# Recommendation tower on one core: ScalarE takes row numbers off the ids in place, one-hots compare with a constant, layer 2's activation stands earlier in ScalarE's order

## The chip, the core and the metric

The kernel runs on one core of one Trainium2 chip. The core's engines work side by side from queues of their own and meet at semaphores: TensorE (PE in the rows; PEld is its weight loads), VectorE (DVE), ScalarE (ACT), GpSimd (POOL, which here only issues the indirect gathers) and SyncE (SP, which issues the plain DMAs). The metric is the device time of one execution in microseconds (us).

## What is computed

A batch of 2048 items. For each item 26 rows of 128 numbers are looked up in 26 tables, and together with the item's dense row they make 27 vectors. All pairs of vectors are multiplied (351 dot products), and a three-layer network runs over the result:

```
e = jnp.stack([tbl_0[ids[:, 0]], ..., tbl_25[ids[:, 25]]], axis=1)
all_vecs = jnp.concatenate([dense_proj[:, None, :], e], axis=1)        # 2048 x 27 x 128
interactions = jnp.einsum('bnd,bmd->bnm', all_vecs, all_vecs)
interact_flat = interactions[:, rows, cols]                           # upper triangle, 351
z = jnp.concatenate([dense_proj, interact_flat], axis=1)
h = jnp.concatenate([z, r_dense_proj], axis=1)
h = jnp.maximum(h @ W_top1 + b_top1, 0.0)     # 607 x 512
h = jnp.maximum(h @ W_top2 + b_top2, 0.0)     # 512 x 256
y = h @ W_top3                                # 256 x 1
```

## The kernel before

The batch is cut into 16 tiles of 128 items, and two tiles make a pair (8 pairs of 256 items). Tile t = 2 * pair + j, with j = 0 or 1.

**Lookups by matmul.** Eleven tables have 1000 rows. These lie in SBUF whole, as a high and a low part (`look_hi`, `look_lo`): row r of a table is on partition r // 8, in chunk r % 8. For one table and one pair, DVE makes eight one-hot matrices of 125 x 256, one for each chunk: element (p, b) is 1 where the id of item b is row 8 p + chunk. They are made in two units of four (`make_unit`, L592), one instruction each (L599), by comparing the ids, which a DMA broadcasts to all partitions as int32 (`step_ids`), with a column of row numbers (`row_no`, 128 x 8). PE then multiplies a unit's four chunks by the high and the low part (L378, L380): 8 matmuls a unit, 22 units a pair. Tile j = 0 of a pair makes and uses the 12 units of tables 0 to 5 of the *next* pair, tile j = 1 the 10 units of tables 6 to 10. The one-hots have 6 slots, so DVE is at most 5 or 6 units ahead of PE. ACT copies what has been looked up out of PSUM (`take_looked`, L717: L728, L734, L738, L740) and merges it into the tile's vectors (L748).

**The other 15 tables** are gathered by POOL with indirect DMAs (L316, 240 of them), turned by PE (L333) and copied by ACT (L572). `gram` (L450) multiplies the vectors, DVE turns the result (`turn`, L576: L579, L585, L588), PE turns the pairs once more (`pairs_out`, L385: L391), and ACT copies them (L698).

**The network** runs once a pair, a pair behind: `layer1` (L422) half in tile j = 0 and half in tile j = 1, `layer2` (L429) in the middle of tile j = 1, `layer3` (L440) at its end. ACT does the activations: `relu1` (L702), `relu2` (L706 and L707), `result` (L713).

**Order.** Each engine's order is written out by hand, tile by tile (`tile` in each engine's block); waits on semaphores tie them together. In the order of ACT, a tile copies groups 0 and 1 of the next tile's gathered rows, then pairs, dense rows and merges, `unit(3)`, group 2 of the rows ("third copy of rows"), `unit(7)`, group 3, and in tile j = 1 after that `relu2` and the last unit. The order of PE in tile j = 1: layer 1's second half, units and turns, first half of `gram`, layer 2, units and turns of groups 2 and 3, more units, second half of `gram`, layer 3. In the next tile j = 0, PE does two units, turns groups 0 and 1 and the dense rows, and then `pairs_out`, which waits for DVE's `turn` of the tile before; in DVE's order this `turn` stands behind the first 6 of 12 units of tile j = 0.

**Start.** Before tile 0 the eleven tables come in one after another by DMA (`load_table`), each behind the 128 KB of its ids (`load_first_ids`). ACT makes the high part (`take_high`, L789), DVE the one-hots and the low part (`take_low`, L609); tables 8 to 10 are first used unsplit (L375). Pairs 1 to 6 then run in a loop (`Fori(1, pairs - 1)`), and the last pair is written out. The ids of a later step come by `load_step` (SP, L244: 768 or 640 KB), once DVE has used up those in the buffer.

Of the kernel before, what the change touches and what calls it, by code (L numbers as in the profile page):

```python
# [33 lines left out]
F32 = mybir.dt.float32  # L34
# [65 lines left out]
def build(nc, dense, ids, look_ids, tables, look_tables, w1_dense, w1_pairs, b1, w2, b2, w3,  # L100
# [7 lines left out]
    with ExitStack() as ctx:  # L108
# [26 lines left out]
        row_no = sb("row_no", [P, LOOK_CH])  # L135
# [45 lines left out]
        gathered = [[sem(f"gathered{j}_{h}") for h in range(2)] for j in range(2)]  # L181
        first_ids_in = [sem(f"first_ids_in{f}") for f in range(LOOKUPS)]
# [47 lines left out]
        with nc.Block() as block:  # L230

            @block.sync
            def _(sp):
# [5 lines left out]
                def load_step(a, pair):  # L239

                    lo, hi = TABLES_OF[a]
                    sp.wait_ge(onehot_made, unit_count(pair - 1, 2 * hi - 1))
                    src = look_ids[lo:hi, bass.ds(pair * PAIR, PAIR)]
                    sp.dma_start(step_ids[a][:, :, :],  # L244
                                 src.unsqueeze(0).broadcast_to([P, hi - lo, PAIR])).then_inc(step_ids_in[a], 16)
# [44 lines left out]
                with sp.Fori(2, pairs) as r:  # L290
                    load_step(0, r)
                    load_step(1, r)
                    load_dense(2 * r, 0)
                    load_dense(2 * r + 1, 1)
                sp.wait_ge(y_out, 16 * (pairs + 1))
# [279 lines left out]
            def _(dve):  # L575
# [15 lines left out]
                def make_unit(a, pair, g, f, half):  # L591
# [5 lines left out]
                    for c in range(UNIT_CH):  # L597
                        ch = half * UNIT_CH + c
                        last = nc.vector.tensor_scalar(  # L599
                            onehot[:, SLOT[g], c, :], step_ids[a][0:LOOK_K, f - TABLES_OF[a][0], :],  # L600
                            row_no[0:LOOK_K, ch:ch + 1], None, ALU.is_equal)
# [10 lines left out]
                def tile(t, j, pair, first=False, look=True):  # L612
# [8 lines left out]
                    if look:  # L621
                        dve.wait_ge(step_ids_in[j], 16 * (pair + 1))
# [13 lines left out]
                dve.wait_ge(row_no_in, 16)  # L636
                for s in range(2):
                    for g, f, half in units(s):
                        if half == 0:
                            dve.wait_ge(first_ids_in[f], 16)  # L640
# [37 lines left out]
            def _(act):  # L678
# [71 lines left out]

                def tile(t, j, pair, first=False, mlp=True, look=True):
# [20 lines left out]
                    unit(3)  # L772
                    copy(n, k, 2)
# [6 lines left out]
                    if mlp and j == 1:  # L780
                        relu2(pair - 1)
# [9 lines left out]
                act.dma_start(row_no[:, :], row_numbers).then_inc(row_no_in, 16)  # L791
# [3 lines left out]
                ahead = LOOKUPS // 2  # L795
                for k in range(ahead):
                    take_high(k)
                for s in range(2):
                    for i, (g, f, half) in enumerate(units(s)):
# [8 lines left out]
                        if half == 1 and f + ahead < LOOKUPS:  # L808
                            take_high(f + ahead)
                tile(0, 0, 0, first=True, mlp=False)  # L810
# [64 lines left out]
```

## Times and profile before

| what | value |
|---|---|
| runs of the kernel before | 455.69, 456.03, 465.37 us; median 456.03 |
| the profiled execution | 457.95 us, its span 455.8 us |
| granted TensorE clock, mean over the span | 0.933 of full speed |
| busy over the span: PE | 385.5 us (85%) |
| PEld | 347.8 us (76%) |
| DVE | 254.1 us (56%) |
| ACT | 146.5 us (32%) |
| POOL | 230.8 us (51%) |
| chain that ended last | PE 72%, issue 10%, another core or an unknown queue 6%, DMA 3%, ACT 3%, SPq 3%, DVE 2% |

A row of the profile names the line of the kernel, the engine, the operation, what it writes and reads, and how often. Times are from the start of the span. In a timeline, the square brackets say how long the engine sat idle before the row, and what released it. "issue" is a wait for nothing that the profile shows, and "remote" is a releaser that it can't name. Full clock is 2.4 GHz (1.00 in the rows), half is 1.2 GHz (0.50).

### The profile page before, as it was taken

How to read it: one execution, taken by the hardware profiler on the slowest of the kernel's cores; microseconds unless marked ns; L12 is line 12 of the kernel's file. 1: busy time of each engine (PE TensorE's matmuls, PEld its weight loads, DVE VectorE, ACT ScalarE, POOL GpSimd, SP SyncE). 2: the span in 40 equal slices, each digit the busy share in tenths (PEclk: the TensorE clock that was granted, in tenths of full speed). 3: DMA queues.
4: the chain of work that ended last, by engine and by line, in shares of the span. 5: the costliest groups of instructions: out<-in, count | busy, mean ns of one | idle time of the engine just before them, and what ended most of it. 6: DMA issues, size and time to landing. Idle time of an engine off the chain costs nothing.

```text
span 455.8 us, 14934 instructions
## 1 busy us (share of the span) xinstructions
PE 385.5 (85%) x6224; PEld 347.8 (76%) x6224; DVE 254.1 (56%) x767; ACT 146.5 (32%) x265; POOL 230.8 (51%) x244
## 2 busy tenths in 40 slices
PE   0779858778898879997889799997999799997977
PEld 0779737767797779895879789885988689885865
DVE  5997729575654375466655466457754457441110
ACT  2264111321513233233424233233504224234422
POOL 4456737566555446545555556555455456551000
PEclk9979969898899989998999979997999979997999
DMA  8999812333251714324141714424151511110000
GB/s 195 239 249 209 233 41 59 98 59 87 61 94 46 91 45 66 84 47 92 42 102 40 104 46 60 91 51 87 41 106 37 95 54 40 40 35 19 3 3 0
DMA packets 25441, 36.37 MB, mean 80 GB/s; under 512 B 5378, under 2 KB 19594, under 8 KB 25417
## 3 DMA queue, kind: packets, MB, share of 16 engines
q1 hardware_dynamic: 17577, 20.27, 24.5%
q0 software_dynamic: 7680, 15.74, 12.7%
q8 instruction: 18, 0.29, 0.3%
q14 instruction: 6, 0.05, 0.0%
q10 hardware_dynamic: 160, 0.01, 0.0%
HBM read 35.99 MB, written 0.01 MB: 79 GB/s over the span
## 4 chain that ended last, share of the span: by engine, by line
PE 72%; issue 10%; another core or an unknown queue 6%; DMA 3%; ACT 3%; SPq 3%; DVE 2%; DVEq 0%; ACTq 0%
PE hid L422 11%; PE gram L450 9%; PE look_ps L378 8%; PE look_ps L380 7%; PE vec_act L333 6%; PE look_odd L380 5%; PE look_odd L378 5%; PE hid L429 5%; PE hid L378 4%; PE hid L380 3%; DMA table_raw<-tbl 3%; PE small L440 2%; DVE onehot L599 2%; PE look_odd L375 2%
## 5 line engine op out<-in xcount | busy, mean ns | idle before, releaser
L316 POOL DMA_INDIRECT vecs<-tbl,ids_sb x240 | 230.6, 961 | 181.2 <-issue 98.7
L599 DVE TENSOR_SCALAR onehot<-step_ids,row_no 125x256 fp32r<-125x256 int32 x704 | 209.8, 360 | 149.1 <-PE look_ps L380 48.2
L378 PE MATMUL look_ps<-onehot,look_hi 125*128 125x256 f32 x312 | 88.2, 313 | 8.4 <-issue 4.5
L380 PE MATMUL look_ps<-onehot,look_lo 125*128 125x256 f32 x312 | 83.5, 298 | 5.4 <-issue 5.3
L572 ACT COPY vecs_T<-vec_act 128x512 f32<-128x512 f32 x64 | 37.9, 600 | 138.7 <-remote 72.3
L450 PE MATMUL gram<-vecs_T 128*27 128x26 f32 x4096 | 52.6, 196 | 27.2 <-issue 27.2
L450 PEld LDWEIGHTS gram<-vecs_T 128*27 128x27 f32 x4096 | 45.4, 107 | 37.1 <-issue 33.4
L378 PEld LDWEIGHTS look_ps<-onehot,look_hi 125*128 125x128 f32 x312 | 64.6, 207 | 10.5 <-issue 5.7
L380 PEld LDWEIGHTS look_ps<-onehot,look_lo 125*128 125x128 f32 x312 | 64.6, 207 | 6.2 <-issue 6.0
L378 PE MATMUL look_odd<-onehot,look_hi 125*128 125x256 f32 x240 | 64.0, 300 | 3.3 <-issue 3.2
L380 PE MATMUL look_odd<-onehot,look_lo 125*128 125x256 f32 x240 | 60.2, 284 | 2.6 <-issue 2.5
L378 PE MATMUL hid<-onehot,look_hi 125*128 125x256 f32 x128 | 41.4, 347 | 11.4 <-DMA ident<-identity 10.8
L380 PEld LDWEIGHTS look_odd<-onehot,look_lo 125*128 125x128 f32 x240 | 45.8, 191 | 4.7 <-issue 4.1
L378 PEld LDWEIGHTS look_odd<-onehot,look_hi 125*128 125x128 f32 x240 | 45.8, 191 | 3.3 <-issue 2.9
L378 PEld LDWEIGHTS hid<-onehot,look_hi 125*128 125x128 f32 x128 | 30.5, 238 | 15.8 <-DMA ident<-identity 10.8
L422 PE MATMUL hid<-pairs_T,w_sb 117*128 117x256 f32 x168 | 40.9, 378 | 0.0
L333 PE MATMUL vec_act<-ident,vecs 128*128 128x128 f32 x240 | 39.1, 288 | 2.1 <-DMA vecs<-tbl,ids_sb 2.1
L380 PE MATMUL hid<-onehot,look_lo 125*128 125x256 f32 x128 | 38.5, 325 | 0.0
L422 PEld LDWEIGHTS hid<-pairs_T,w_sb 117*128 117x128 f32 x168 | 31.8, 189 | 4.5
L333 PEld LDWEIGHTS vec_act<-ident,vecs 128*128 128x128 f32 x240 | 29.9, 149 | 3.3 <-DMA vecs<-tbl,ids_sb 2.3
L380 PEld LDWEIGHTS hid<-onehot,look_lo 125*128 125x128 f32 x128 | 30.5, 238 | 0.0
L702 ACT ACTIVATE h_T<-hid 128x512 f32<-128x512 f32 x14 | 8.4, 598 | 65.0 <-remote 34.8
(80 smaller groups left out, 320.5 us busy)
## 6 DMA issues: line engine op xcount, KB each, us to landing
step_ids<-look_ids SPq DMA_DIRECT2D x7, 768.0 KB
table_raw<-tbl SPq DMA_DIRECT2D x11, 448.0 KB
step_ids<-look_ids SPq DMA_DIRECT2D x7, 640.0 KB
vecs<-tbl,ids_sb POOLq DMA_INDIRECT x240
step_ids<-look_ids SPq DMA_DIRECT2D x11, 128.0 KB, 9.6
vecs<-dense SPq DMA_DIRECT2D x16, 64.0 KB
table_raw<-tbl SPq DMA_DIRECT2D x11, 52.0 KB
w_sb<-w SPq DMA_DIRECT2D x1, 512.0 KB
```

Source lines behind the costliest of these rows:

```text
L316: nc.gpsimd.indirect_dma_start(out=vecs[j][:, 1 + k, :], out_offset=None, in_=tables[k], in_offset=bass.IndirectOffsetOnAxis(ap=ids_sb[:, ...
L333: last = nc.tensor.transpose(vec_act[q_bank(j, q)][:, v, :], vecs[j][:, 1 + row, :], ident[:, :])
L375: last = nc.tensor.matmul(bank, table_raw[:, f, ch, :], onehot[:, SLOT[g], c, :].bitcast(F32), start=ch == 0, stop=ch == LOOK_CH - 1)
L378: nc.tensor.matmul(bank, look_hi[:, f, ch, :], onehot[:, SLOT[g], c, :], start=ch == 0, stop=False)
L380: last = nc.tensor.matmul(bank, look_lo[:, f, ch, :], onehot[:, SLOT[g], c, :], start=False, stop=ch == LOOK_CH - 1)
L422: last = nc.tensor.matmul(hid1[:, o, :], *operand, start=c == 0, stop=c == CHUNKS)
L429: last = nc.tensor.matmul(hid2[:, o, :], *layer2_operand(o, c), start=c == 0, stop=c == H1 // P - 1)
L440: last = nc.tensor.matmul(bank, w3_sb[:, c:c + 1], h2_T[:, c, :], start=c == 0, stop=c == H2 // P - 1)
L450: last = nc.tensor.matmul(gram[s * QUAD:s * QUAD + VECS, g, 0:2 * FOLD], v[:, 0:VECS], v.rearrange("d (h n) -> d h n", h=2)[:, :, 0:FOLD], ...
L572: return engine_copy(vecs_T[j][:, :, 1 + lo:1 + hi], bank[:, 0:hi - lo, :].rearrange("d v b -> d b v"))
L599: last = nc.vector.tensor_scalar(onehot[:, SLOT[g], c, :], step_ids[a][0:LOOK_K, f - TABLES_OF[a][0], :], row_no[0:LOOK_K, ch:ch + 1], Non ...
L702: nc.scalar.activation(h1_T[:, 2 * half:2 * half + 2, :], hid1[:, :, :], ACT.Relu).then_inc(h1_copied, 1)
```

## The change

Three things are changed together.

1. ACT takes each partition's first row number (8 p) off the ids, in place: `shift_ids` is an Identity activation with a bias `row_first` (128 x 1, holding -8 p), from int32 to fp32 in the same bytes of `step_ids`. It runs once for each table in the start (11 times on 125 x 256), once in front of tile 0, and once in each tile up to the loop's end (on 125 x 1280 or 125 x 1536). DVE now waits for ACT's `ids_shifted` where it waited for the DMA of the ids.
2. The one-hot compares the shifted ids with a constant (`float(ch)`) and no longer with a column of `row_no`.
3. In tile j = 1, `relu2` moves from behind `copy(n, k, 3)` to in front of `copy(n, k, 2)`.

SP loads the ids of tables 0 to 5 of the last pair once more at the end, so that the shift in the loop's last pass has its count.

```
-        row_no = sb("row_no", [P, LOOK_CH])
+        row_first = sb("row_first", [P, 1])
...
+        ids_shifted = sem("ids_shifted")
...
-                def load_step(a, pair):
+                def load_step(a, pair, cols=None):
...
-                    src = look_ids[lo:hi, bass.ds(pair * PAIR, PAIR)]
+                    src = look_ids[lo:hi, bass.ds((pair if cols is None else cols) * PAIR, PAIR)]
...
+                load_step(0, pairs, pairs - 1)
                 sp.wait_ge(y_out, 16 * (pairs + 1))
...
                         last = nc.vector.tensor_scalar(
-                            onehot[:, SLOT[g], c, :], step_ids[a][0:LOOK_K, f - TABLES_OF[a][0], :],
-                            row_no[0:LOOK_K, ch:ch + 1], None, ALU.is_equal)
+                            onehot[:, SLOT[g], c, :], step_ids[a][0:LOOK_K, f - TABLES_OF[a][0], :].bitcast(F32),
+                            float(ch), None, ALU.is_equal)
...
                     if look:
-                        dve.wait_ge(step_ids_in[j], 16 * (pair + 1))
+                        dve.wait_ge(ids_shifted, LOOKUPS + t + 1)
...
-                dve.wait_ge(row_no_in, 16)
                 for s in range(2):
                     for g, f, half in units(s):
                         if half == 0:
-                            dve.wait_ge(first_ids_in[f], 16)
+                            dve.wait_ge(ids_shifted, f + 1)
...
+                def shift_ids(a, lo, hi):
+                    rows = step_ids[a][0:LOOK_K, lo:hi, :]
+                    nc.scalar.activation(rows.bitcast(F32), rows, ACT.Identity,
+                                         bias=row_first[0:LOOK_K, 0:1]).then_inc(ids_shifted, 1)
+                def shift_first(f):
+                    a = f // FIRST_TABLES
+                    act.wait_ge(first_ids_in[f], 16)
+                    shift_ids(a, f - TABLES_OF[a][0], f - TABLES_OF[a][0] + 1)
+                def shift_step(a, pair):
+                    act.wait_ge(step_ids_in[a], 16 * pair)
+                    shift_ids(a, 0, TABLES_OF[a][1] - TABLES_OF[a][0])
...
                     unit(3)
+                    if look:
+                        shift_step(k, pair + 1 + j)
+                    if mlp and j == 1:
+                        relu2(pair - 1)
                     copy(n, k, 2)
                     unit(7)
                     copy(n, k, 3)
...
-                    if mlp and j == 1:
-                        relu2(pair - 1)
                     unit(UNITS_OF[j] - 1)
...
+                act.wait_ge(row_no_in, 16)
+                shift_first(0)
                 for k in range(ahead):
                     take_high(k)
+                    shift_first(k + 1)
...
                         if half == 1 and f + ahead < LOOKUPS:
                             take_high(f + ahead)
+                        if half == 1 and f + ahead + 1 < LOOKUPS:
+                            shift_first(f + ahead + 1)
+                shift_step(0, 1)
                 tile(0, 0, 0, first=True, mlp=False)
...
-        "row_numbers": np.arange(P * LOOK_CH, dtype=np.float32).reshape(P, LOOK_CH),
+        "row_numbers": np.arange(0, -P * LOOK_CH, -LOOK_CH, dtype=np.float32).reshape(P, 1),
```

The order of instructions shows the places. Line numbers of the changed kernel are its own (L757 is the shift, L811 `take_high`, L575 the copy of rows, L602 the one-hot).

First place, ACT in the start, from the high part of the eighth table on. Before:

```order
L789 CAST look_hi<-table_raw 125x1024 x2
L572 COPY vecs_T<-vec_act 128x128x4
L572 COPY vecs_T<-vec_act 128x128x3
L689 COPY dense_new<-small 128x128
L690 COPY vecs_T<-small 128x128
L728 COPY vecs_T<-look_ps 128x2x256
```

And in the changed kernel:

```order
L811 CAST look_hi<-table_raw 125x1024
L757 ACTIVATE step_ids<-step_ids,row_first 125x256
L575 COPY vecs_T<-vec_act 128x128x4
L575 COPY vecs_T<-vec_act 128x128x3
L691 COPY dense_new<-small 128x128
L692 COPY vecs_T<-small 128x128
L730 COPY vecs_T<-look_ps 128x2x256
```

Between table 7's high part and the copies of tile 0's rows there is now the shift of table 8's ids.

Second place, ACT from the last lookup of the start into tile 0. Before:

```order
L728 COPY vecs_T<-look_odd 128x2x256
L728 COPY vecs_T<-look_ps 128x256
L572 COPY vecs_T<-vec_act 128x128x4
L572 COPY vecs_T<-vec_act 128x128x3
L689 COPY dense_new<-small 128x128
```

Changed:

```order
L730 COPY vecs_T<-look_odd 128x2x256
L730 COPY vecs_T<-look_ps 128x256
L757 ACTIVATE step_ids<-step_ids,row_first 125x1536
L575 COPY vecs_T<-vec_act 128x128x4
L575 COPY vecs_T<-vec_act 128x128x3
```

The shift of the six tables' ids that tile 0 needs stands behind the copy (L728, now L730) of the last table looked up in the start.

Third place, ACT in tile j = 1 of the loop, from the copies of `unit(3)` on. Before:

```order
L740 COPY looked_late<-look_ps 128x256
L680 REGISTER_ALU
L572 COPY vecs_T<-vec_act 128x128x4
L726 REGISTER_ALU
L738 COPY vecs_T<-look_odd 128x2x128
L740 COPY looked_late<-look_odd 128x256
L680 REGISTER_ALU
L572 COPY vecs_T<-vec_act 128x128x4
L706 ACTIVATE h_T<-hid,b_sb 128x256
L707 ACTIVATE h_T<-hid,b_sb 128x256
```

Changed:

```order
L742 COPY looked_late<-look_ps 128x256
L768 ISA
L757 ACTIVATE step_ids<-step_ids,row_first 125x1536
L708 ACTIVATE h_T<-hid,b_sb 128x256
L709 ACTIVATE h_T<-hid,b_sb 128x256
L682 REGISTER_ALU
L575 COPY vecs_T<-vec_act 128x128x4
L728 REGISTER_ALU
L740 COPY vecs_T<-look_odd 128x2x128
L742 COPY looked_late<-look_odd 128x256
```

The two activations of layer 2 no longer stand behind the copies of `unit(7)` and of group 3; in front of them stands the shift of the next ids.

## Rows read from the trace of the kernel before

**Rows 1.** Stretch of the loop: length, busy by engine, PEclk, DMA share, GB/s.
```profile
300.00:340.00 40.00, 36.11 (x588) 32.75 (x587) 24.60 (x80) 13.15 (x25) 22.43 (x24) 0.91 0.35 71
```
**Rows 2.** Timeline, 308 to 322: start, length, engine, line, [idle before <- releaser].
```profile
310.87 1.36 PE L450 MATMUL gram<-vecs_T 128*27 128x26 f32 x122 [1.19 <-issue]
...
310.98 5.39 DVE L599 TENSOR_SCALAR onehot<-step_ids,row_no 125x256 fp32r<-125x256 int32 x16 [1.09 <-remote]
...
313.44 1.87 PE L440 MATMUL small<-h_T,w_sb 128*1 128x256 f32 x4 [1.20 <-ACT h_T L707]
...
318.13 0.40 DVE L588 COPY_PREDICATED pair_rows_sb<-mask,gram_rows 128x169 f32<-128x169 int32 x1 [0.16 <-issue]
...
320.01 0.49 PE L391 MATMUL small<-ident,pair_rows_sb 128*117 128x128 f32 x3
```
**Rows 3.** Waits: who for whom, us in total, times, longest.
```profile
PE small L440 <- ACT h_T L707: 4.7, 4, 1.2
```
**Rows 4.** Timeline, 150 to 170: the loop's first pass at the same place.
```profile
154.86 7.40 DVE L599 TENSOR_SCALAR onehot<-step_ids,row_no 125x256 fp32r<-125x256 int32 x24 [9.03 <-PE look_odd L380]
...
157.84 1.02 PE L440 MATMUL small<-h_T,w_sb 128*1 128x256 f32 x4 [0.20 <-issue]
...
164.46 0.59 PE L391 MATMUL small<-ident,pair_rows_sb 128*117 128x128 f32 x3 [2.62 <-DVE pair_rows_sb L588]
```
**Rows 5.** Short stretches of PE: length, busy, then granted clock, DMA share, GB/s.
```profile
313.00:314.00 1.00, 0.56 (x2) 0.50 0.02 8
415.00:416.00 1.00, 0.26 (x24) 0.50 0.00 0
```
**Rows 6.** Groups of DVE by line: busy us, mean ns of one | idle before.
```profile
L599 DVE TENSOR_SCALAR onehot<-step_ids,row_no 125x256 fp32r<-125x256 int32 x704 | 209.8, 360 | 149.1 <-PE look_ps L380 48.2 <-PE look_odd L380 35.0 <-remote 34.8
L609 DVE TENSOR_TENSOR look_lo<-table_raw,look_hi 125x1024 fp32r<-125x1024 f32 x11 | 13.5, 1224 | 1.4 <-ACT look_hi L789 1.1
L654 DVE TENSOR_TENSOR w_sb<-w_sb,h_T 128x512 f32<-128x512 f32 x1 | 0.7, 672 | 0.0
```
**Rows 7.** The one-hot instructions: shortest, median and longest in ns.
```profile
L599 DVE TENSOR_SCALAR onehot<-step_ids,row_no x704: 332/348/585, 5.1 to 405.3; 125x256 fp32r<-125x256 int32 x176
```
**Rows 8.** Groups of ACT by line, the nearest to the new shifts.
```profile
L748 ACT COPY vecs_T<-looked 128x768 f32<-128x768 f32 x14 | 24.4, 1740 | 0.0
L789 ACT CAST look_hi<-table_raw 125x1024 fp32r<-125x1024 f32 x11 | 11.5, 1048 | 21.4 <-DMA table_raw<-tbl 17.1 <-issue 4.3
L706 ACT ACTIVATE h_T<-hid,b_sb 128x256 f32<-128x256 f32 x7 | 3.4, 491 | 2.6 <-PE hid L429 2.6
```
**Rows 9.** Timeline of the start, 28 to 41.
```profile
29.39 1.05 ACT L789 CAST look_hi<-table_raw 125x1024 fp32r<-125x1024 f32 x1 [2.13 <-DMA table_raw<-tbl]
...
32.94 0.55 PE L378 MATMUL look_ps<-onehot,look_hi 125*128 125x256 f32 x1 [2.40 <-ACT vecs_T L728]
...
34.51 1.23 DVE L609 TENSOR_TENSOR look_lo<-table_raw,look_hi 125x1024 fp32r<-125x1024 f32 x1
```
**Rows 10.** The stretch behind PE's idle time in the start.
```profile
33.00:34.00 1.00, 1.00 (x5) 0.50 0.99 228
```
**Rows 11.** Timeline, 41 to 66: into tile 0.
```profile
45.60 7.47 DVE L599 TENSOR_SCALAR onehot<-step_ids,row_no 125x256 fp32r<-125x256 int32 x24 [0.28 <-issue]
...
49.69 0.65 ACT L728 COPY vecs_T<-look_ps 128x256 f32<-128x256 f32 x1 [2.34 <-PE look_ps L375]
...
50.01 0.39 PE L378 MATMUL hid<-onehot,look_hi 125*128 125x256 f32 x1 [0.36 <-issue]
...
64.44 0.37 PE L380 MATMUL look_ps<-onehot,look_lo 125*128 125x256 f32 x1 [1.01 <-issue]
```
**Rows 12.** Timeline of ACT in tile j = 1, 298 to 306.
```profile
300.93 0.48 ACT L740 COPY looked_late<-look_ps 128x256 f32<-128x256 f32 x1
...
305.20 0.58 ACT L572 COPY vecs_T<-vec_act 128x512 f32<-128x512 f32 x1 [3.79 <-PE vec_act L333]
```
**Rows 13.** Timeline of ACT in tile j = 0, 270 to 279.
```profile
275.95 0.59 ACT L572 COPY vecs_T<-vec_act 128x512 f32<-128x512 f32 x1 [1.22 <-PE vec_act L333]
```

More of the change, by code:

```diff
@@ L789, in take_high @@
                     nc.scalar.copy(look_hi[:, f, :, :], table_raw[:, f, :, :]).then_inc(table_high, 1)
-                act.dma_start(row_no[:, :], row_numbers).then_inc(row_no_in, 16)
+                act.dma_start(row_first[:, :], row_numbers).then_inc(row_no_in, 16)
                 act.sem_inc(y_out, 16)
```

## The prediction

> **What bounds the kernel now.** I read the stretches first: in the loop PE is busy for 36.1 of 40 us, DVE for 24.6, ACT for 13.2 [rows 1]. So PE sets the pace there, and cheaper work on DVE or ACT pays only where PE waits for it. Next I looked in the list of waits and in the timeline for what PE's idle time ends with. Much of it is "issue", which this change doesn't touch. Two waits are of its making. PE sits idle for 1.20 us in front of layer 3, until layer 2's second activation is done (L707), which happens 4 times for 4.7 us [rows 2, 3]. And in the loop's first pass PE sits idle for 2.62 us in front of `pairs_out`, until DVE's turn is done [rows 4]; DVE had been released at 154.86 and first had 24 one-hots to make. In later passes this second wait doesn't show, and the reader is to see why. With the clock at half, PE comes to `pairs_out` (L391) 6.57 us after layer 3's start (313.44 to 320.01), and DVE is done at 318.13 + 0.40 = 318.53, which is 1.48 us ahead [rows 2]. In the first pass, at full clock, PE was there after 4.0 us (157.84 to 164.46 less 2.62) and had to wait [rows 4]. The start is another regime: there PE waits for ACT, which waits for the tables' DMAs [rows 9].
>
> **The one-hot.** It takes 348 ns in the median and 360 in the mean, and there are 704 [rows 6, 7]. The trace shows no DVE instruction with a constant on this tile, so the new price is bounded. Two subtracts give a line for DVE at its plain rate: 1224 ns for 1024 elements and 672 for 512, so 1.08 ns an element and 120 ns fixed [rows 6]. By it 256 elements take 396 ns, more than the 348 measured, so the one-hot already runs faster per element. If that is two elements at a time, 138 + 120 = 258 ns would be left, and the other 90 ns belong to what is special in it: the column operand, the int32 source, or the fast rate itself. So 258 from below, and 348 (nothing gained) from above. I take 290, near the middle and a little lower, because both the column and the int32 source go: 58 ns less each. The Trainium skill, page "VectorE: DVE Perf Modes", section "The TRN2 errata — SBUF-src ops pay a fixed extra latency per instruction", measures a fixed part of about 150 cycles; with 128 ticks for 256 elements at 0.96 GHz that is an estimate of 290 ns, and no instruction here shows it at this rate. In its section "Rules for kernel authors" the page says to minimize the number of DVE ops and not to fuse them; the number here stays.
>
> What the 58 ns are worth: 41 us of DVE's time, nearly all hidden under PE. It counts where DVE is waited for: in the first pass 24 x 0.058 = 1.4 us of the 2.62. In later passes it moves the end of DVE's turn forward by 16 x 0.058 = 0.9 us.
>
> **The shift on ACT.** In the loop it costs ACT some 3 us a pair. ACT's nearest rows: 491 ns for 256 elements with a bias, 1048 for 1024, and 1740 for 768 in a strided copy [rows 8]. The first two give 0.73 ns an element, so 1.4 us for 1536 contiguous elements and 1.2 for 1280; at the strided row's 2.27 ns it would be 3.5 us. The shift is contiguous, so I take 1.5 and 1.3. In tile j = 1 it lies behind L740, which ends at 301.41, and in front of a copy that starts at 305.20 after 3.79 us of idleness: shift 1.5 and both activations 1.0 fit [rows 12]. In tile j = 0 there are 1.22 us of idleness at 275.95 and the shift takes 1.3, so that copy moves by 0.1 us [rows 13]. DVE's first one-hot behind it is due at about the same moment, so nothing is lost. If the shift took 3.5 us, the copies would move by 1 to 2 us, for which PE doesn't wait at once.
>
> **The shift in the start** is not hidden, at two places. Table 8's shift, 0.5 us, now stands between L789 (29.39) and the copies that PE waits for until 32.94 [rows 9]: +0.5, and up to +1.6 if these ids land late. Then tile 0. Before, DVE began tile 0's one-hots at 45.60, and PE used the first at 50.01, as soon as it was through with the start [rows 11]. Now ACT shifts tile 0's ids only after the last copy of the start (49.69 + 0.65 = 50.34). Then 1.5 for the shift and 1.1 for four one-hots: PE starts at 53.0, which is +3.0. Such idle time also brings the clock down: after 2.40 us idle in the start the next stretch is at half clock [rows 9, 10]. Three microseconds at half lose up to 1.5; I take 1.3, since the one-hots pace PE there anyway. Sum for the start: 0.5 + 3.0 + 1.3 = +4.8 us. The upper end is 0.5 + 1.1 + 3.0 + 2.0 (shift at 3.5) + 1.5 = 8.1. The lower end is near 0: PE crawls with waits on "issue" until about 65 [rows 11], and if these belong to a moment of time and not to a place in PE's program, they swallow the delay.
>
> **relu2.** Moved forward, it is done about 8 us before layer 3. The waits named go: 4.7 us. It has a second effect if the clock stays up. In the stretch from 313 on the clock is at half [rows 5]. At full clock PE would come to `pairs_out` in 4.0 instead of 6.57 us, 1.2 + 2.57 = 3.8 us earlier; but DVE is done with its turn only 1.48 + 0.9 = 2.4 us earlier than needed now. So 2.4 and not 3.8, and the wait of the first pass (row L391) appears in each. Does the clock stay? Against it: from 415.00 on it is at half throughout, while PE works there until 415.26 and its wait begins only then [rows 5], so the idle time before, in `gram` (1.19 us at 310.87 [rows 2] and the like), can do it alone. For it: in the first pass layer 3 ran at full clock, 1.02 against 1.87 us, with 0.20 us of wait [rows 2, 4]. The Trainium skill, page "TensorE: Matmul & The Clock Gate", says that throttled is the default and activity releases it; so less idle time can only help, but it doesn't settle how much is enough. I take two of the four passes as kept, at 2.4 - 1.2 = 1.2 more each.
>
> **The sum.** +4.8 (start) - 1.4 (first pass) - 4.7 (four waits) - 2.4 (clock, two passes) = -3.7. The profiled execution took 457.95 us, so 454.2. The median of the runs shown is 456.03, which is 1.9 less than the profiled one, so I forecast **452.3**, within 2% of before, which is about what a measurement of this kernel can tell from no change. The extra load at the end costs nothing: no engine but ACT's last shift asks for it, and it has a whole tile to land.
>
> **Rivals.**
> - *The clock stays up in every pass.* For it speaks the first pass, against it 415. Start +4.8; first pass -1.4 and -1.3, since the wait that remains there is too short to bring the clock down; three passes at 2.4; the last one, which has no one-hots in front of its turn, 3.6; the second pass 1.4 for its slow layer 3 and the units behind it. Together -10.1: 446.
> - *The one-hot doesn't get cheaper,* since its extra 90 ns belong to the fast rate. Then the first pass gives nothing and a kept clock only 0.3 more a pass: +4.8 - 4.7 = 0: 456.
> - *The start's delay is swallowed* by the crawl behind it: -8.5 from the loop alone: 447.5.
> - *The one-hot gets dearer: slower.* If with a constant it lost the fast rate, it took 396 to 416 ns; take 68 more. Each table of the start costs DVE 8 x 0.068 = 0.54 us, 4.4 up to the end of the low part that starts at 34.51 [rows 9], which PE needs almost at once: +4.2 in place of +0.5. Then +3.3 into tile 0 and +1.3 for the clock, +1 for one-hots slower than PE's units there, +1.6 in the first pass, and only 2.3 of the 4.7 are won, since DVE's turn comes 1.1 us later. Sum +9.1: 465. Against it speaks that source and target stay in SBUF with the same shape. It decides from the present 348 ns on: every price above that makes a kernel slower than before.
>
> **Chances.** My forecast 0.44, the clock up everywhere 0.24, no cheaper one-hot 0.14, the start swallowed 0.07, a dearer one-hot 0.06, other 0.05. Faster by over 2% means below 446.9: most of the clock case and a third of the swallowed start, 0.23. Slower by over 2% means above 465.2: half of the dear case and part of the rest, 0.06. Within 2%: 0.71. The range takes in the first four cases, 444.5 to 458.5; its upper end lies 2.5 above no gain, for a late table 8 and a slow shift. The forecast's own range is 449 to 456.
>
> **What would show it.** The one-hot's median: 290 is right, 348 the second rival, near 400 the last. PE's first matmul of tile 0 at about 53.5, released by DVE. No idle time in front of layer 3 in the loop. The granted clock behind it: full in about half the passes, and where it is full, a wait of 1 us or more in front of L391's successor, released by DVE. ACT's shift at 1.3 and 1.5 us. I would be wrong if waits on "issue" grew or fell by several us (they are a tenth of the chain), or if DVE now waited for ACT's shift in each tile.

## The result and the profile after

| | before | after |
|---|---|---|
| median of 20 runs each, taken in turns on one chip | 458.24 us (455.66 to 465.6) | 455.4 us (452.34 to 459.54) |
| profiled execution, its span | 457.95, 455.8 | 455.78, 453.8 |
| ratio of after to before | | 0.995, 95% interval 0.9927 to 0.9973 |

The change makes the kernel 0.5% faster by the ratio, 2.3 us; by the medians it is 2.8 us. The forecast was 452.3 us, which is 3.1 us too low. All ratios here are made from those executions of a kernel that lie within 1.5% of its fastest.

From the page of the kernel after: busy time by engine, the granted clock in 40 slices, the chain, two groups of instructions.

```profile
PE 379.7 (84%) x6224; PEld 344.0 (76%) x6224; DVE 212.9 (47%) x767; ACT 171.6 (38%) x291; POOL 236.2 (52%) x244
...
PEclk9978988888999999998999989999999988998999
...
PE 79%; issue 12%; DMA 3%; SPq 3%; DVE 1%; ACT 1%; another core or an unknown queue 0%; DVEq 0%
...
L602 DVE TENSOR_SCALAR onehot<-step_ids 125x256 fp32r<-125x256 f32 x704 | 168.5, 301 | 185.5 <-PE look_ps L383 57.3
...
L453 PE MATMUL gram<-vecs_T 128*27 128x26 f32 x4096 | 53.0, 198 | 33.3 <-issue 33.2
```

DVE has 41.2 us less to do (254.1 before) and ACT 25.1 more (146.5). PE's waits on "issue" in front of `gram` have grown from 27.2 us to 33.2. Line numbers have moved by 2 or 3: the one-hot is L602 (L599 before), layer 3 L443 (L440), `pairs_out` L394 (L391), the second activation L709 (L707).

The new shifts are three groups of ACT in the kernel after, by shape (behind the first bar: busy us, mean ns):

```profile
L757 ACT ACTIVATE step_ids<-step_ids,row_first 125x1536 f32<-125x1536 int32 x8 | 12.8, 1602 | 0.0
L757 ACT ACTIVATE step_ids<-step_ids,row_first 125x1280 f32<-125x1280 int32 x7 | 9.6, 1368 | 0.0
L757 ACT ACTIVATE step_ids<-step_ids,row_first 125x256 f32<-125x256 int32 x11 | 5.6, 509 | 0.3
```

The timeline of after at the place of [rows 2]:

```profile
311.42 1.33 PE L453 MATMUL gram<-vecs_T 128*27 128x26 f32 x119 [1.19 <-issue]
311.49 0.67 ACT L740 COPY vecs_T<-look_odd 128x256 f32<-128x256 f32 x1 [5.96 <-remote]
311.49 4.17 DVE L602 TENSOR_SCALAR onehot<-step_ids 125x256 fp32r<-125x256 f32 x16 [2.00 <-remote]
...
312.82 1.02 PE L443 MATMUL small<-h_T,w_sb 128*1 128x256 f32 x4
...
317.42 0.39 DVE L591 COPY_PREDICATED pair_rows_sb<-mask,gram_rows 128x169 f32<-128x169 int32 x1 [0.16 <-DVE pair_rows_sb L588]
...
317.86 0.59 PE L394 MATMUL small<-ident,pair_rows_sb 128*117 128x128 f32 x3 [1.04 <-DVE pair_rows_sb L591]
```

The 1.20 us in front of layer 3 are gone, layer 3 runs at full clock (1.02 against 1.87 us), and PE now waits 1.04 us for DVE's turn a little later, as the forecast had it for a pass in which the clock stays up. But that is so in this one of the last five passes: in the others layer 3 still takes 1.8 us or so, with no wait on the relu in front of it. There the clock falls behind waits on "issue" in `gram`.

A ledger shows where the difference stands. Layer 3's products occur six times in the loop, so the first and the last start of that row in a trace split the span in three: what comes before the first, the five pass lengths between, and the rest. Slow and fast mean the chip: the kernel before took 458.24 us in the comparison above and 461.09 in the last group of experiments (slow), but 397.59, 396.74 and 396.43 us in the three groups between, each on another chip (fast). Each line is one execution. The slow before and after come from the comparison, the other slow ones from the last group, which has no trace of the kernel before.

| kernel | chip | up to first layer 3 | five passes | rest | span |
|---|---|---|---|---|---|
| before | slow | 157.8 | 259.8 | 38.2 | 455.8 |
| after | slow | 162.3 | 254.0 | 37.5 | 453.8 |
| relu2_third | slow | 157.2 | 258.4 | 39.3 | 454.9 |
| shift_third | slow | 161.5 | 256.8 | 40.2 | 458.5 |
| start_third | slow | 158.7 | 253.3 | 38.2 | 450.2 |
| few_ids_third | slow | 157.9 | 256.5 | 38.2 | 452.6 |
| before_again | fast | 140.8 | 215.8 | 39.8 | 396.4 |
| after_again | fast | 145.2 | 215.2 | 38.1 | 398.5 |
| relu2_again | fast | 138.4 | 215.8 | 38.0 | 392.2 |
| start_again | fast | 136.4 | 215.2 | 38.1 | 389.7 |
| few_ids_before | fast | 132.3 | 215.9 | 39.5 | 387.7 |
| few_ids_after | fast | 134.0 | 215.1 | 37.8 | 386.9 |

So after against before: +4.5, -5.8, -0.7, in sum -2.0 of the span. Pass by pass, from the start of one layer 3 to the next, the five are 1.9, 1.8, 1.4 and 1.1 us shorter, and the last is 0.4 us longer (52.1 against 51.6). In that last pass `gram` of after stands twice on "issue", and then the clock falls a second time, at a place where it stays up before:

```profile
373.85 0.25 PE L453 MATMUL gram<-vecs_T 128*27 128x26 f32 x4 [1.20 <-issue]
375.26 0.95 PE L453 MATMUL gram<-vecs_T 128*27 128x26 f32 x64 [1.16 <-issue]
```

The granted clock from 376 to 377 us is 0.50 in after and 1.00 in before. Over the whole stretch from 150 to 425 us, PE is at half clock for 34.2 us before and for 17.1 us after. The clock falls five times there in place of six, and stays down for a shorter time.

### The profile page after: what moved, and what is told of

Read it like the earlier page. It is cut to its first block, busy times and chain, and to the rows that moved or that the text cites. A ratio compares the mean times of both kernels' runs of the same rounds, so it can differ in the third digit from the quotient of the medians.

```text
span 453.8 us, 14973 instructions
## 1 busy us (share of the span) xinstructions
PE 379.7 (84%) x6224; PEld 344.0 (76%) x6224; DVE 212.9 (47%) x767; ACT 171.6 (38%) x291; POOL 236.2 (52%) x244
## 3 DMA queue, kind: packets, MB, share of 16 engines
q1 hardware_dynamic: 18361, 21.05, 27.2%
## 4 chain that ended last, share of the span: by engine, by line
PE 79%; issue 12%; DMA 3%; SPq 3%; DVE 1%; ACT 1%; another core or an unknown queue 0%; DVEq 0%
PE hid L425 11%; PE gram L453 11%; PE look_ps L381 9%; PE look_ps L383 9%; PE look_odd L381 7%; PE look_odd L383 6%; PE vec_act L336 6%; PE hid L432 6%; PE hid L381 3%; DMA table_raw<-tbl 3%; PE hid L383 3%; PE small L443 2%; PE look_odd L378 2%; SPq L259 1%; PE small L394 1%
## 5 line engine op out<-in xcount | busy, mean ns | idle before, releaser
L319 POOL DMA_INDIRECT vecs<-tbl,ids_sb x240 | 236.0, 983 | 175.6 <-issue 101.9
L602 DVE TENSOR_SCALAR onehot<-step_ids 125x256 fp32r<-125x256 f32 x704 | 168.5, 301 | 185.5 <-PE look_ps L383 57.3
L453 PE MATMUL gram<-vecs_T 128*27 128x26 f32 x4096 | 53.0, 198 | 33.3 <-issue 33.2
L453 PEld LDWEIGHTS gram<-vecs_T 128*27 128x27 f32 x4096 | 46.8, 110 | 40.9 <-issue 37.0
L575 ACT COPY vecs_T<-vec_act 128x512 f32<-128x512 f32 x64 | 37.8, 599 | 101.4 <-remote 53.2
L381 PE MATMUL look_odd<-onehot,look_hi 125*128 125x256 f32 x240 | 65.2, 305 | 3.0 <-issue 2.9
L381 PE MATMUL hid<-onehot,look_hi 125*128 125x256 f32 x128 | 37.5, 323 | 14.4 <-DMA ident<-identity 11.0
L381 PEld LDWEIGHTS hid<-onehot,look_hi 125*128 125x128 f32 x128 | 27.3, 213 | 18.4 <-DMA ident<-identity 11.0
L383 PE MATMUL hid<-onehot,look_lo 125*128 125x256 f32 x128 | 34.9, 303 | 0.0
L582 DVE STREAM_TRANSPOSE gram_rows<-gram 128x832 f32<-128x832 f32 x15 | 15.7, 1043 | 26.6 <-PE gram L453 26.6
```

Of the source, the lines that this page charges most:

```text
L319: nc.gpsimd.indirect_dma_start(out=vecs[j][:, 1 + k, :], out_offset=None, in_=tables[k], in_offset=bass.IndirectOffsetOnAxis(ap=ids_sb[:, ...
L381: nc.tensor.matmul(bank, look_hi[:, f, ch, :], onehot[:, SLOT[g], c, :], start=ch == 0, stop=False)
L383: last = nc.tensor.matmul(bank, look_lo[:, f, ch, :], onehot[:, SLOT[g], c, :], start=False, stop=ch == LOOK_CH - 1)
L453: last = nc.tensor.matmul(gram[s * QUAD:s * QUAD + VECS, g, 0:2 * FOLD], v[:, 0:VECS], v.rearrange("d (h n) -> d h n", h=2)[:, :, 0:FOLD], ...
L575: return engine_copy(vecs_T[j][:, :, 1 + lo:1 + hi], bank[:, 0:hi - lo, :].rearrange("d v b -> d b v"))
L582: nc.vector.transpose(gram_rows[:, :, :, :].rearrange("p h n m -> p (h n m)"), gram[:, :, 0:2 * FOLD].rearrange("p g n -> p n g")).then_in ...
```

## Experiments

Sixteen runs followed, in four groups of four; some kernels ran in several groups, on other chips. The sum could have failed in two ways: the start could cost more, or the waits that go could come back. So the change was first taken apart.

**The relu alone.** The kernel before with this edit:

```
                     unit(3)
+                    if mlp and j == 1:
+                        relu2(pair - 1)
                     copy(n, k, 2)
                     unit(7)
                     copy(n, k, 3)
...
-                    if mlp and j == 1:
-                        relu2(pair - 1)
```

> The kernel before with layer 2's activation moved alone: no shift, one-hots against the column. Theory of the sum (each part is worth what it is worth alone): the four idle stretches of 1.2 us before layer 3 go, so the time falls by 4.7 us, to about 0.990 of before, and the time that layer 3 starts in the loop's last pass (416.39 before) comes 4 to 6 us earlier. Rival, the waits on 'issue' are dealt out anew whenever an engine's pace changes: the idle time before layer 3 goes all the same, but the sum of PE's waits on 'issue' (about 43 us before, 52 us in the changed kernel) grows by several us and the time falls by less than 2.5 us (over 0.994).

Measured: 398.59 us, ratio 1.0019 (0.9968 to 1.0071). The surprise was the level: on this chip the kernel before takes 397.59 us, 13% less.

**The shift and the constant alone** are the changed kernel with the relu back in its old place.

> The changed kernel with layer 2's activation back in its old place: the shifts and the constant one-hots alone. Theory of the sum: +4.8 us in the start less 1.4 us in the loop's first pass, so +3.4 us, 1.007 of before; PE's wait before layer 3 (1.2 us, four times) is back. Rival, the start's delay is swallowed by PE's crawl behind tile 0's first units, and only the 1.4 us gained are left: 0.997 of before or no difference.

Measured: 400.2 us, 0.9969 (0.9898 to 1.0039), which decides nothing.

**The first pass's shift early.** The changed kernel shifts tile 0's ids after the last copy of the start; here that one statement stands at the start's second turn:

```
+                        if s == 1 and i == SECOND_TURN + 1:
+                            shift_step(0, 1)
...
-                shift_step(0, 1)
```

> The changed kernel with the shift of tile 0's ids moved forward in ScalarE's order, behind the copies of the second turn in the start (about 45 us) and no longer behind the last lookup's copy. If the delay of tile 0 (PE's first one-hot matmul at 54.14 against 50.01 before) costs its full 3 us to the end, this kernel is 3 us (0.7%) faster than the changed one: 0.988 of before, and PE begins tile 0 at 51.2. If the crawl swallows it, PE begins tile 0 at 51.2 too, but the turn of the dense rows that follows the crawl's end (86.84 in the changed kernel, 85.49 before) stays where it is within 1 us, and so does the time.

Measured: 395.84 us, 0.9972 (0.9929 to 1.0016).

**The start as before.** In addition the one-hots of the start read int32 and compare with the old column, so ACT shifts nothing there but tile 0's ids.

> The changed kernel with the start's one-hots made as before (int32 ids against the column, no shift of single tables) and the shift of tile 0's ids early, at about 45 us; constants and shifts from tile 0 on, and layer 2's activation moved. By the sum nothing of the start's +4.8 us is left: -1.4 and -4.7 and up to -2.4 for the clock, so 450 to 452 where before is 458 (0.983 to 0.987). PE begins table 6 at 32.9 and tile 0 at 50.0, as before. If the start's delay was swallowed anyway, it equals the changed kernel (0.995).

Measured: 393.67 us, 0.9949 (0.9908 to 0.9991): the first version that is faster than before on this kind of chip with the interval below 1. Both last kernels come to layer 3 at the same moment (137.1 and 136.9 us in their traces), so the eleven small shifts cost little; the one of tile 0 is what counts.

**The same four places again, with the kernels before and after beside them.**

> The kernel before once more, for its profile. Two chips so far gave it 458 us and 397 us. Theory A (the waits that the sum priced come from the stalls of the slower chip): where it takes some 397 us, TensorE waits on 'issue' for under 12 us in all, layer 3's products (L440) wait for the second relu (L707) for under 1 us in all, and all 24 of them run at the full clock (0.38 us each); where it takes some 458 us, 'issue' is 40 us or more and L440 waits for L707 3 to 6 us. Rival B (the wait on the second relu belongs to the program): L440 waits for L707 some 4.7 us in both. Ratio to itself 1.000.

Measured: 397.34 us, 0.9994 (0.9957 to 1.0032). In its trace, the rows of the tile `small` (shortest, median and longest in ns, first and last start) and all that PE waited for in front of them:

```profile
L440 PE MATMUL small<-h_T,w_sb x24: 376/377/379, 140.8 to 356.6; 128*1 128x256 f32 x24
...
its engine sat idle before it (us, times) until:
  DVE pair_rows_sb L588: 1.0, 4
```

No wait on the relu at all, where [rows 3] has 4.7 us, and all 24 products at full clock. Theory A holds, rival B falls: the waits that I had priced are no property of the program alone. On the slow chip PE waits on "issue" for over 40 us, here for 7.4, and the slow trace at the place of [rows 2] shows what a relu has to do with it:

```profile
310.98 0.69 ACT L738 COPY vecs_T<-look_odd 128x256 f32<-128x256 f32 x1 [5.19 <-remote]
...
312.59 0.51 ACT L707 ACTIVATE h_T<-hid,b_sb 128x256 f32<-128x256 f32 x1
```

ACT's three copies ahead of the relu begin only at 310.98, after 5.19 us of idleness, just when PE comes out of such waits (310.87). Those copies, and the relu behind them, are then late for layer 3.

> The changed kernel once more. Theory A: on a chip where the kernel before takes some 397 us the relu gives nothing, the cheap one-hots give the 4 us of DVE's turn back (pair_rows_sb waits under 1 us in place of some 4 us) and the late start costs 3 us: ratio 0.995 to 1.002. On a chip where it takes some 458 us: ratio 0.993 to 0.997 as measured before. Rival B: 0.990 or less on a chip of 397 us, since 4.7 us of waits would go out of a shorter span.

Measured: 401.07 us, 1.0021 (0.9955 to 1.0087). Eleven of its twelve executions took 399.5 to 403.9 us and one 394.2; by the medians the ratio would be 1.011. No gain is shown either way. The profiled one is one of the eleven (400.35 us), and what follows on its start is read from such an execution. It has a wait that before_again doesn't have:

```profile
96.37 0.96 PE L453 MATMUL gram<-vecs_T 128*27 128x26 f32 x65 [6.02 <-issue]
```

The changed kernel with the relu back, which has the same start, shows it on its own chip too, at the same product (4.81 us in e2_shift_only). column_fp32 below, again with this start, doesn't: it has 3.55 us at a later product.

> The kernel before with the second relu in front of the third copy, and nothing else. The chip of 397 us gave 1.002 (0.997 to 1.007). Theory A: there again 0.997 to 1.003; on a chip of 458 us 0.988 to 0.993, since four waits of 1.2 us go (4.7 us of 458). Rival C (a wait that goes is dealt out again as 'issue' waits): 0.997 to 1.003 on a chip of 458 us too, with 'issue' of TensorE 4 us or more above that of the kernel before on the same chip.

Measured: 398.36 us, 1.002 (0.9973 to 1.0068). Twice nothing, as there is no wait to take away.

> The changed kernel, but its start works as before: the one-hots of the look-ups ahead of the first pass compare the ids as int32 with the column of row numbers, and ScalarE's shift begins with the first pass's ids, done early. The chip of 397 us gave 0.995 (0.991 to 0.999). Theory A: 0.993 to 0.997 again there, 3 to 4 us (0.7 to 1%) under the changed kernel of the same call; on a chip of 458 us 0.982 to 0.988. Rival D (the late start is swallowed later): the same as the changed kernel of the same call within 0.3%.

Measured: 392.11 us, 0.9884 (0.9814 to 0.9954). It has four executions. That is 1.4% under the changed kernel of the same group by the ratios and 2.2% by the medians. Rival D falls on this chip: the ledger has 8.8 us between the two before the first layer 3 (145.2 and 136.4), more than the 3 to 4 us that the late start is worth by itself.

**What the late start runs into.** I read the 6.02 us above as a late fetch of PE's code. Two queues are marked "instruction". q8 moves 18 packets of 16 KB in an execution, nearly all before the loop and behind it, and I take it for PE's; q14 moves 6. From 84 to 94 us of after_again the transfers stand so, with no packet on q8 (and one on q14):

```profile
DMA  2234333033449904999997959999998996898987
...
q1 hardware_dynamic: 799, 0.72, 68.7%
```

From 81 to 94 there is just one on q8, before 82; the next comes between 94.0 and 94.5, while PE is already standing (from 90.35 to 96.37). In e2_shift_only q8 is as empty from 85 to 94 us. All that time queue q1 is busy. It carries the ids of the next pair, 768 or 640 KB in small packets. So the loads of ids were cut, in both kernels, to 16 of 128 partitions:

```
-                    sp.dma_start(step_ids[a][:, :, :],
-                                 src.unsqueeze(0).broadcast_to([P, hi - lo, PAIR])).then_inc(step_ids_in[a], 16)
+                    sp.dma_start(step_ids[a][0:16, :, :],
+                                 src.unsqueeze(0).broadcast_to([16, hi - lo, PAIR])).then_inc(step_ids_in[a], 16)
```

> The kernel before, but each of its loads of look-up ids (768 KB and 640 KB on SP's queue) writes 16 of the 128 partitions: an eighth of the bytes; the ids of the other partitions are whatever lay there, so the looked-up rows are not the reference's, the work is the same. Theory E (gathers and code fetches of the first 100 us queue behind these loads): TensorE's wait for gathered rows of some 6.9 us at 68 to 75 us and that of 2.5 us go, 'issue' falls from some 7 us; 385 to 390 us on the chip of 397. Rival F (they are late for another reason): 394 us or more with the wait of 6 to 7 us in its place.

> The changed kernel with the same cut of its loads of ids to 16 of 128 partitions (its looked-up rows are not the reference's). Theory E: the wait of some 6 us in gram at 90 to 96 us, labelled issue, goes, and what is left between this kernel and the one before with the same cut is the start's own 3 to 5 us less 1.4 us of one-hots: 1 to 4 us above it. Rival F: the 6 us stay. Rival G (the start's delay is hidden once nothing collides): equal to the kernel before with the same cut, within 1 us, or below it.

Measured: 389.23 us (0.9829, 0.9792 to 0.9866) and 389.42 us (0.9848, 0.9809 to 0.9888), both against the uncut kernel before. The transfers of few_ids_after from 84 to 94 us, with a code packet among them, and the `gram` in question without a wait:

```profile
DMA  4871006500036000180001630008200054000350
...
q1 hardware_dynamic: 191, 0.11, 3.7%
...
q8 instruction: 1, 0.02, 0.8%
```

```profile
88.22 1.84 PE L453 MATMUL gram<-vecs_T 128*27 128x26 f32 x128
```

Theory E holds in its main point: without the heavy loads the code packet comes in time and the 6.02 us are gone, and the wait of 6.93 us for gathered rows that before_again has at 68.5 us goes too. The executions of either kernel now lie within 3.2 us of each other, where after_again's spread over 9.7. But the two kernels are equal, as rival G said; theory E had 1 to 4 us for the start. The ledger between them: +1.7, -0.8, -1.7.

**What made the one-hot dear.**

> The kernel before, but the one-hots compare with a constant and still read int32; nothing shifts the ids, so the row's part of the id is left out and the looked-up rows are not the reference's. If the column operand alone is what made the one-hot dear: median 286 ns. If the int32 source alone is: 348 ns. If both have a part: between, some 310 to 320 ns.

> The changed kernel, but the one-hots compare the shifted fp32 ids with a column that holds the same number in all partitions, in place of a constant. If the column operand alone is the price: median 348 ns. If the int32 source alone was: 286 ns. If both have a part: between.

The one-hots of int32_const and of column_fp32 (shortest, median, longest in ns):

```profile
L599 DVE TENSOR_SCALAR onehot<-step_ids x704: 273/286/525, 5.0 to 340.4; 125x256 fp32r<-125x256 int32 x176
```

```profile
L603 DVE TENSOR_SCALAR onehot<-step_ids,row_no x704: 332/348/553, 6.3 to 346.8; 125x256 fp32r<-125x256 f32 x176
```

The column is the whole price, 62 ns; int32 costs nothing. The single executions took 391.49 and 397.38 us.

**On a slow chip again.** In the fourth group the kernel before takes 461.09 us. All four ratios of this group lie between 0.992 and 0.995, though the edits differ, and their intervals overlap; so they can't say what one edit is worth against another.

> The kernel before with the relu moved, alone. On a chip of 458 us: theory A (four waits of 1.2 us go) 0.988 to 0.993; rival C (they are dealt out again as issue waits) 0.997 to 1.003. On a chip of 397 us both say 0.997 to 1.003.

Measured: 457.04 us, 0.9938 (0.9886 to 0.999). The interval reaches into both claims, so the trace has to decide. PE's waits first, and then the place where the clock fell and relu2 was waited for in the kernel before:

```profile
PE gram L450 <- issue: 29.5, 39, 2.4
...
PE small L391 <- DVE pair_rows_sb L588: 6.5, 3, 2.3
```

```profile
260.25 4.12 DVE L599 TENSOR_SCALAR onehot<-step_ids,row_no 125x256 fp32r<-125x256 int32 x12
260.28 1.02 PE L440 MATMUL small<-h_T,w_sb 128*1 128x256 f32 x4
...
264.29 1.04 DVE L579 STREAM_TRANSPOSE gram_rows<-gram 128x832 f32<-128x832 f32 x1
...
266.13 0.39 DVE L588 COPY_PREDICATED pair_rows_sb<-mask,gram_rows 128x169 f32<-128x169 int32 x1 [0.16 <-issue]
...
266.57 0.59 PE L391 MATMUL small<-ident,pair_rows_sb 128*117 128x128 f32 x3 [2.27 <-DVE pair_rows_sb L588]
```

No wait on the relu, and layer 3 at full clock. But PE, 1.2 us and more earlier, meets DVE, which has twelve one-hots of 348 ns in front of its turn, and waits 2.27 us. And the clock, which had stayed up, falls now. The stretches 266:267, 267:268 and 268:269 (the clock is the third figure from the end):

```profile
266.00:267.00 1.00, 0.43 (x4) 0.43 (x5) 0.87 (x4) 0.08 (x1) 0.69 (x2) 1.00 0.16 45
267.00:268.00 1.00, 1.00 (x10) 1.00 (x9) 0.96 (x4) 0.42 (x1) 0.81 (x1) 0.82 0.25 66
268.00:269.00 1.00, 1.00 (x6) 1.00 (x6) 0.70 (x3) 0.00 (x0) 0.89 (x1) 0.50 0.40 102
```

So the wait moved by six microseconds, and its clock loss with it (for before see [rows 5]). The five passes take 258.4 us against 259.8. Neither claim has the mechanism: the relu's 4.7 us came back as waits for DVE's turn, three times and 6.5 us in all, in later passes that have none of them before. (The first pass's wait, 2.62 us before, stands here under "issue" with 2.49.) What is left as gain is the clock: from 150 to 425 us PE is at half for 20.5 us, not 34.2.

> The changed kernel with the relu back behind the third copy. On a chip of 458 us: theory A 1.003 to 1.008 (start's 3 to 4 us, less 1.4), and L443 waits for the relu 3 to 6 us in all; rival C 0.995 to 0.998, as the changed kernel. On a chip of 397 us: 0.997 to 1.003, no wait on the relu.

Measured: 457.26 us, 0.9944 (0.9894 to 0.9995). In its trace the relu is still waited for:

```profile
PE small L443 <- ACT h_T L709: 3.2, 3, 1.2
```

and the passes take 256.8 us. Theory A had 1.003 to 1.008 for the time, and the delay of the start doesn't show in it, though the trace has it (161.5 at the first layer 3). The profiled execution took 460.52 us, 3.3 above the median. Against the trace of before, the two edits alone have 1.4 and 3.0 us less in the five passes, both together 5.8. That fits the view that each clears the way for the other, but it isn't shown: these are single executions from two groups, and few_ids_third, which has neither edit, has 3.3 us less too.

> The changed kernel with the start of before and an early shift of the first pass's ids. On a chip of 458 us 0.982 to 0.988 if the start's delay is still there at the end, 0.993 to 0.997 if the stalls swallow it. On a chip of 397 us 0.987 to 0.995, as twice before.

Measured: 454.75 us, 0.9923 (0.9883 to 0.9964), the lowest time of the group. Its span is 3.6 us below that of after, as much as it is ahead at the first layer 3, but the profiled execution is the shortest of its ten (452.03). The ratio lies between the two claims (0.982 to 0.988 and 0.993 to 0.997), and the interval reaches into the second and not into the first. How much of the start's delay the stalls swallow isn't settled: 0.9923 here and 0.995 of the changed kernel have overlapping intervals.

> The kernel before with loads of ids cut to 16 of 128 partitions (looked-up rows not the reference's). On a chip of 458 us: if the trains of stalls at gram come from these loads, issue falls from 43 us to under 10 and the time to 400 to 415 us; if not, 448 to 455 us and issue stays above 35 us. On a chip of 397 us 0.983 (0.979 to 0.987) as before.

Measured: 456.76 us, 0.9945 (0.9902 to 0.9989). PE's waits on "issue" are 40.7 us in all, where the one claim had under 10 and before has 43.5. Two of the waits:

```profile
PE gram L450 <- issue: 25.4, 37, 2.3
...
PE small L440 <- ACT h_T L707: 4.9, 5, 1.1
```

So the trains of stalls are not made by the loads of ids, and the waits on the relu stay with them. Where they come from stays open.

## Why the prediction was right or wrong

**The conversion to the median: wrong, the largest part of the 3.1 us.** I took 1.9 us off because the median of the three runs shown was that much below the profiled one. With 20 runs the median is 458.24, 0.3 above the profiled 457.95, so the step should have added 0.3. Three runs between 455.69 and 465.37 could not carry it.

**The one-hot: right.** 290 ns taken, 286 measured [rows 7]. The Trainium skill, page "VectorE: DVE Perf Modes", section "The TRN2 errata — SBUF-src ops pay a fixed extra latency per instruction", has a fixed part of about 150 cycles; the estimate of 290 ns worked out from it agrees with the trace. My reason was half wrong: int32 has no part in it. So ACT's shift to fp32 only serves to take off the row number.

**The shift: right.** 1.5 and 1.3 us taken; 1.60 and 1.37 in the mean. Nothing in the loop waits for it: of DVE's waits on it there are two, 4.5 us in all, and both lie in the start.

**The start: +4.8 forecast, +4.5 measured up to the first layer 3.** The size is right, but it came about by other means, and that is luck. PE began tile 0 at 54.14, not 50.01: +4.1 for the forecast's 3.5. Then the crawl did swallow most of it, 3 us, as the third rival said: the `gram` behind it begins at 68.28 against 67.14 [rows 11 show the crawl]. But at two later places PE now stood on "issue", as I read it for want of code. The timeline of after:

```profile
120.96 0.25 PE L453 MATMUL gram<-vecs_T 128*27 128x26 f32 x6 [1.82 <-issue]
...
134.93 0.93 PE L453 MATMUL gram<-vecs_T 128*27 128x26 f32 x84 [2.42 <-issue]
```

The first of these waits was 0.35 us before, the second did not exist: before, a packet moved on q8 between 120 and 130 us, after, none; it is in the stretch 132.4:134 instead, in which PE stands:

```profile
q8 instruction: 1, 0.02, 3.9%
```

I had no term for this. It is 3.9 us here and 6.0 in the trace of a fast chip. The Trainium skill, page "Runtime: NRT & Kernel Launch", section "Instruction fetch mechanics", says that code is refilled in 16 KB blocks by the engine's own queue, and that crossing a boundary is mostly hidden. The blocks are as it says; in this kernel's start the hiding failed at these places, if my reading is right, and on the fast chip it held once the loads were cut (few_ids_after).

**The loop: -8.5 forecast, -5.8 measured. Here the sum of the terms failed.** The first pass's turn, the relu's waits and the clock (-1.4, -4.7, -2.4) all lie in the five passes. The first pass's wait for DVE's turn fell from 2.62 to 1.27 us, which is 1.35 for the 1.4, and that pass is 1.9 us shorter. The four waits on the relu are gone [rows 3]. But the four passes that had them are only 3.9 us shorter in sum, where the terms for them, 4.7 and 2.4, make 7.1. The clock's term failed: layer 3 was at full clock in one of the four passes, not in two, and in that one the forecast's wait behind it appeared, 1.04 us. And the relu's term wasn't kept whole: PE's waits on "issue" in the five passes grew from 19.5 to 23.7 us (1.27 of it is the first pass's wait, under another label), and in the last pass the clock fell once more and took the gain away. The lower clock did get less time, 17.1 us for 34.2, but not where I had priced it. The relu's waits themselves exist only on a chip that stalls: before_again has none.

**The rest, 0.7 us less,** has no term; this part varies from 37.5 to 40.2 us in the ledger without an order that would fit the edits. In sum: -3.7 forecast, -2.0 measured in the span. Of the difference of 1.7, the start is -0.3, the loop +2.7 and the rest -0.7. So a gain outside every term hides part of the loop's miss.

**One general flaw** is behind the loop's terms: I priced waits one by one with all else fixed. I had named a change of several us in the waits on "issue" as what would prove me wrong, and they grew from 43.5 to 52.5 us: by 4.1 up to the first layer 3 (there 3.15 us are the wait for tile 0's one-hots, which the trace labels so, and 3.9 what I take for code, while other stalls shrank), by 4.2 in the five passes and by 0.6 behind them. Why the stalls grew in the loop stays open.

## What to carry to other kernels

- A wait that goes may be worth no more than the distance to the next engine's turn on the same path; ask who is late next and whether that wait brings the clock down in its place. With the relu moved alone, 4.7 us of waits went and 6.5 us of waits for DVE came (relu2_third).
- A late instruction in the start can cost more than its own delay where code or gathered rows come behind large loads: 8.8 us for 3 to 4 in the traces of one fast chip. With the shift of tile 0 ahead of the start's last copies and the start's one-hots as before, the change beat the kernel before in all of three comparisons (0.9949, 0.9884, 0.9923).
- Compare with a constant where you can: a column operand took DVE 348 ns, a constant 286, whatever the source's type. Convert between a profiled time and a median only with many runs.

## What the runs showed of the hardware

- The same program takes 396 to 398 us on some chips and 458 to 461 on others. PE's waits on "issue" are 7.4 us in before_again and 43.5 in before. The five passes take 215.1 to 215.9 us in each of the ledger's traces on a fast chip, whatever the edit, and 253.3 to 259.8 on a slow one.
- The waits on the slow chips come in trains, three or four in a pass, in the products of `gram` and of the lookups alike (of before: 285.95 `gram`, 297.52 lookup, 310.87 `gram`, 337.24 `gram`, 348.75 lookup, 362.22 `gram`). When they end, other engines start within 0.1 us of PE: 311.42 PE, 311.49 ACT, 311.49 DVE above, and the lookup whose result ACT copies there had ended before 308. The trains are still there with the loads of ids cut (few_ids_third), and no packet moves on q8 from 170 to 415 us of before, so it is not PE's code if q8 is its queue. The cause is open.
- The granted clock falls behind such a wait, or behind the wait on DVE that takes its place, once in nearly every pass of the slow chips (mean over the span 0.92 to 0.955), and in no pass from 150 to 360 us of before_again or after_again.
